# Unread matmuls in TensorE's waits, six small transfers issued by GpSimd, and a later scale exchange in a two-layer conditional FFN kernel

## The chip, the cores and the metric

The kernel runs on one core of a Trainium2 chip. The metric is device time in microseconds (us) of one execution, as a median over runs. Engines are named as the profile names them: PE (TensorE), DVE (VectorE), ACT (ScalarE), POOL (GpSimd), SP (SyncE, here only an issuer of DMAs).

## The reference

`x` is 64 batches of 64 channels by 1024 positions, in fp32. Two layers are added to it, each a small mixing followed by a matmul with a 1024x1024 weight:

```python
# layer 0: an attention over K=8 kernels makes a 64x64 matrix per batch; fp8 quantised FFN
att = softmax(gelu(gelu(cond @ W0 + b0) @ W1 + b1) @ W2 + b2)
mixed = einsum('boi,bih->boh', einsum('bk,koi->boi', att, weight), x) + (att @ bias_k)[:, :, None]
fp8_x, sx = mixed / (amax(|mixed|) / 448) in fp8;  fp8_w, sw = the same of weight.T
x = x + (fp8_x @ fp8_w) * (sx * sw) + bias
# layer 1: a grouped convolution of 9 taps plus a context column; FFN with 4-bit weights, dequantised
y = conv1d(x, weight, groups=4, padding=4) + (cond @ c_weight.T)[:, :, None] + fside[None, :, None]
x = x + y @ ((W_q - zero) * scale).T + bias
```

Both quantisations of layer 0 are over a whole tensor. Nothing can be divided by a scale before its largest absolute value is known: that of the weight (1024x1024), and that of all mixed `x`.

## The kernel before, in words

`x` is 32 tiles of 128 partitions (two batches of 64 channels) by 1024 columns, and all of them stay in the SBUF tensor `Y` (`slot(t)` is tile t). The order on each engine is the order of the code in its block, and semaphores tie the engines together. Three stages follow each other.

The opening (to about 22 us). PE computes the small MLP on `cond`; DVE makes the softmax `att` and splits it in three bf16 parts (`att_parts`). The mixing kernels `cwk` are split by DVE in three bf16 parts `wkp` (`wk_parts` counts: part 0 ready at 1, part 1 at 3, part 2 at 4), and small SBUF to SBUF transfers spread each part over 72 partitions of `wkp9`, three transfers a part. Before, SP issues six of them (parts 0 and 1, semaphore `wkp`, line L336) and GpSimd three (part 2, `wkl`, L462). 32 matmuls (L1030) make the 64x64 matrices of all batches, which ACT (three quarters) and DVE (`place_last`, L792) write into `mixw`, zeroed by DVE in four pieces. DVE also takes the largest absolute value of the eight row blocks of the first weight (`largest_w0`, L757), as `load_w0` brings them.

The scale exchange. The eight block maxima become one column (`w_part`, L827), PE turns it into a row (L1080), DVE reduces it (`w_all`, L834), a matmul with ones spreads it over the partitions (L1053), and DVE computes the scale (`scales`, L782 and L784).

The weight stage (to about 92 us) is eight cycles on DVE: quantise one block of the first weight (L729, L732, L734), take zeros off one block of the second (`less_w1`, L819), take maxima over three mixed tiles (`largest_mixed`, L804; the list `groups` says which tiles one instruction covers). Beside it GpSimd finishes the rounding (`round_w0`, L489) and the scaling (`times_w1`, L483), PE mixes tile after tile (L1047, eight passes of fp32 for two tiles) and transposes weights, and ACT evicts the mixed tiles (L581). A second exchange, over all mixed tiles, follows.

The main stage: tiles 0 to 2 by hand, then a pipelined loop. PE runs the first FFN (L1131, L1141), the convolution (L1157, 48 matmuls a tile) and the second FFN (L1167). Before the first convolution PE turns the quantised tile 2 (`turned_first_q`, L1118) and waits for the shifted copies of tile 0 (`moved_sp`, `moved_pool`, issued at L411 and L532).

## Time and profile before

| | us |
|---|---|
| median of three runs | 531.81 (529.83 to 533.81) |
| the profiled execution, its own time | 531.02 |
| its span | 528.8 |
| PE busy | 508.1 (96%) |
| DVE busy | 414.6 (78%) |
| ACT busy | 244.4 (46%) |
| GpSimd busy | 59.3 (11%) |
| mean granted TensorE clock | 0.994 |

The profile is one execution. The span runs from the first to the last instruction on the core, and the execution's own time is 2.2 us more. Busy shares are averages over all three stages: in the opening and the weight stage DVE has next to no idle time, in the main stage PE. A matmul of fp32 appears as two passes of one count each, so that one tile's mixing is four passes (x4). Durations of single matmuls contain the pipeline's latency; where many follow each other, the total divided by the count is the rate.

### The profile page before, as it was taken

How to read it: one execution, taken by the hardware profiler on the slowest of the kernel's cores; microseconds unless marked ns; L12 is line 12 of the kernel's file. 1: busy time of each engine (PE TensorE's matmuls, PEld its weight loads, DVE VectorE, ACT ScalarE, POOL GpSimd, SP SyncE). 2: the span in 40 equal slices, each digit the busy share in tenths (PEclk: the TensorE clock that was granted, in tenths of full speed). 3: DMA queues.
4: the chain of work that ended last, by engine and by line, in shares of the span. 5: the costliest groups of instructions: out<-in, count | busy, mean ns of one | idle time of the engine just before them, and what ended most of it. 6: DMA issues, size and time to landing. Idle time of an engine off the chain costs nothing.

```text
span 528.8 us, 9418 instructions
## 1 busy us (share of the span) xinstructions
PE 508.1 (96%) x3460; PEld 282.1 (53%) x3460; DVE 414.6 (78%) x524; ACT 244.4 (46%) x286; POOL 59.3 (11%) x68
## 2 busy tenths in 40 slices
PE   2999999979999999999999999999999999999997
PEld 2544454455555555555555555555555555555563
DVE  7899999966877777777777777777777777777652
ACT  3579987844444444444444444444444444442310
POOL 5276665030000000000000000000000000000000
PEclk9999999979999999999999999999999999999999
DMA  7999671244675666665556565655665666666632
GB/s 239 393 385 408 242 283 42 79 92 131 185 198 168 201 184 177 189 180 180 180 180 180 180 180 180 180 180 180 180 180 180 183 182 184 181 188 185 195 120 79
DMA packets 85650, 100.59 MB, mean 190 GB/s; under 512 B 34468, under 2 KB 67046, under 8 KB 85638
## 3 DMA queue, kind: packets, MB, share of 16 engines
q1 hardware_dynamic: 84610, 99.41, 59.6%
q0 software_dynamic: 656, 0.82, 0.9%
q10 hardware_dynamic: 372, 0.20, 0.2%
q8 instruction: 7, 0.11, 0.1%
q14 instruction: 5, 0.04, 0.0%
HBM read 58.41 MB, written 32.75 MB: 172 GB/s over the span
## 4 chain that ended last, share of the span: by engine, by line
PE 79%; DVE 11%; DMA 4%; issue 2%; SPq 1%; ACT 1%; POOL 1%; DVEq 0%; ACTq 0%; POOLq 0%
PE pair L1167 40%; PE pair L1141 19%; PE pair L1157 16%; DVE stat L804 5%; DMA work<-work 2%; DMA Y<-in_L_ffn_weight_dram 2%; PE pair L1047 1%; PE pair L1131 1%; DVE work L729 1%; DVE work L819 1%; DVE Y L819 1%; SPq L336 1%; DVE work L732 1%; POOL fixed L489 1%; DVE work L741 1%
## 5 line engine op out<-in xcount | busy, mean ns | idle before, releaser
L1167 PE MATMUL pair<-f1T,work 128*128 128x512 f16 x1024 | 231.0, 379 | 0.0
L1167 PEld LDWEIGHTS pair<-f1T,work 128*128 128x128 f16 x1024 | 98.9, 98 | 113.4
L608 ACT ACTIVATE work<-Y,consts 128x1024 bf16 (+1 forms) x29 | 33.3, 1148 | 187.0 <-DVE work L902 187.0
L921 DVE TENSOR_TENSOR work<-Y,work 128x512 f16<-128x512 f16 (+1 forms) x64 | 71.3, 1120 | 47.3 <-ACT work L641 46.2
L1141 PE MATMUL pair<-f0T,work 128*128 128x512 bf16 x464 | 104.9, 379 | 0.7 <-DMA work<-work 0.7
L1157 PEld LDWEIGHTS pair<-taps,work 128*128 128x128 f16 x1536 | 90.4, 99 | 10.0 <-issue 2.7
L1157 PE MATMUL pair<-taps,work 128*128 128x128 f16 x1536 | 93.0, 221 | 2.6 <-DMA work<-work 2.6
L934 DVE TENSOR_TENSOR Y<-pair,Y 128x512 f32 (+1 forms) x64 | 44.1, 689 | 44.9 <-PE pair L1167 44.9
L641 ACT CAST work<-Y 128x512 f16 (+1 forms) x64 | 69.7, 1138 | 18.5 <-DVE Y L911 15.6
L1141 PEld LDWEIGHTS pair<-f0T,work 128*128 128x128 bf16 x464 | 45.3, 98 | 55.7 <-DMA work<-work 1.2
L1047 PE MATMUL pair<-Y,work 128*128 128x512 f32 x128 | 62.6, 625 | 1.2 <-DVE work L792 0.8
L646 ACT CAST work<-pair 128x512 f16<-128x512 f32 x64 | 37.4, 585 | 34.9 <-PE pair L1157 33.4
L940 DVE SCALAR_TENSOR_TENSOR pair<-work,consts,fixed 128x512 f32<-128x512 f32 x64 | 48.2, 754 | 0.1
L911 DVE SCALAR_TENSOR_TENSOR Y<-pair,stat,Y 128x512 f32 (+1 forms) x64 | 45.1, 743 | 2.6 <-PE pair L1131 1.4
L928 DVE TENSOR_TENSOR work<-pair,work 128x512 f16<-128x512 f32 x64 | 41.4, 686 | 3.2 <-ACT work L646 3.1
L581 ACT ACTIVATE Y<-pair,consts 128x1024 f32<-128x1024 f32 (+1 forms) x33 | 36.0, 1093 | 13.4 <-PE pair L1047 13.4
L895 DVE SCALAR_TENSOR_TENSOR Y<-work,Y 128x1024 bf16 (+1 forms) x29 | 35.5, 1225 | 4.0
L804 DVE TENSOR_REDUCE stat<-Y 128x1 f32<-128x1024 f32 (+2 forms) x23 | 36.4, 1629 | 0.7 <-ACT Y L581 0.6
L902 DVE SCALAR_TENSOR_TENSOR work<-work,Y 128x1024 bf16<-128x1024 bf16 x29 | 35.5, 1225 | 1.2
L1047 PEld LDWEIGHTS pair<-Y,work 128*128 128x128 f32 x128 | 23.1, 196 | 23.3 <-issue 22.0
L609 ACT ACTIVATE Y<-Y,stat (+1 forms) x29 | 32.9, 1133 | 0.0
L489 POOL TENSOR_TENSOR fixed<-Y,work 128x1024 bf16<-128x1024 f32 x8 | 24.0, 3005 | 19.7 <-DVE Y L734 19.7
(153 smaller groups left out, 229.9 us busy)
## 6 DMA issues: line engine op xcount, KB each, us to landing
Y<-in_x_dram SPq DMA_DIRECT2D x64, 512.0 KB, 3.9
out_dram<-Y SPq DMA_DIRECT2D x31, 512.0 KB, 3.8
split_rows<-work SPq DMA_DIRECT2D x30, 520.0 KB, 2.6
work<-split_rows SPq DMA_DIRECT2D x30, 520.0 KB, 3.9
Y<-in_L_ffn_weight_dram SPq DMA_DIRECT2D x8, 512.0 KB, 5.7
Y<-in_L_ffn_W_q_dram SPq DMA_DIRECT2D x5, 512.0 KB, 13.2
work<-in_L_ffn_W_q_dram SPq DMA_DIRECT2D x3, 512.0 KB, 15.5
work<-work SPq DMA_DIRECT2D x8, 65.0 KB, 3.8
```

Source lines behind the costliest of these rows:

```text
L641: nc.scalar.copy(split[:, r, h:h + S, 0], v[:, r, :]).then_inc(hi_done, 1)
L646: nc.scalar.copy(y1s[n][:, 0, :, b * C:(b + 1) * C].rearrange("p r (g a) -> p g r a", g=G), ps[4 + b][:, :].rearrange("p (g r a) -> p g r ...
L804: nc.vector.tensor_reduce(stat[:, n:n + 1], part, AX.X, ALU.max, apply_absolute_value=True).then_inc(mixed_red, 1)
L911: nc.vector.scalar_tensor_tensor(out=v, in0=ps[h][:, :], scalar=acc_neg, in1=v, op0=ALU.mult, op1=ALU.add).then_inc(x1_done, 1)
L921: nc.vector.tensor_tensor(split[:, r, s, 1], v[:, r, :], split[:, r, s, 0], ALU.subtract)\
L928: nc.vector.tensor_tensor(part(1), ps[4 + b][:, :].rearrange("p (g r a) -> p g r a", g=G, r=R8), part(0), ALU.subtract).then_inc(ylo_done, 1)
L934: nc.vector.tensor_tensor(v, ps[2 + h][:, :], v, ALU.add).then_inc(res_done, 1)
L940: nc.vector.scalar_tensor_tensor(out=ps[2 + h][:, :], in0=wsum[:, c], scalar=ctxcol[:, bass.ds(t, 1)], in1=fixed[:, c], op0=ALU.mult, op1= ...
L1047: last = mm(ps[2 * (t % 2) + h][:, :], mixw[:, t, :], slot(t)[:, h * H:(h + 1) * H], start=True, stop=True)
L1141: last = mm(ps[h][:, :], qT[n][:, k, :], f0T[:, k, h * H:(h + 1) * H], start=(k == 0), stop=(k == KT - 1))
L1157: last = mm(ps[4 + b][:, g * P:(g + 1) * P], convin[:, b * G + g, h:h + S, xp], taps16[:, wp, h, g].rearrange("p r a -> p (r a)"), start=( ...
L1167: last = mm(ps[2 + h][:, :], y1s[n][:, e, k, :], f1T[:, k, h * H:(h + 1) * H], start=False, stop=(e == 1 and k == KT - 1), skip_group_chec ...
```

## The change

Seven edits. (1) Of the nine spreading transfers SP issues three (part 0) and GpSimd six (parts 1 and 2), part 1 as soon as it is ready. (2) GpSimd waits for the four attention parts before it copies the taps. (3) The load of mixed tile 1 moves ahead of the load of weight block 7. (4) `place_last` moves from behind weight block 4's maximum to behind block 1's. (5) In the exchange, PE's transpose moves from behind tile 0 to behind tile 1, its matmul with ones from the middle of tile 1 to the middle of tile 2, the transposes of zeros and scales from behind tile 1 to behind tile 2, and DVE's two sums over the taps from ahead of the row maximum to behind it. (6) In each cycle DVE takes one single tile's maximum ahead of the zeros, and a pair's behind them; before, it took the pair's and the single one's behind. PE's bias matmul goes ahead of the taps' transposes. (7) PE gets matmuls whose results nobody reads: 16, 4 and 8 of 128x128 in the opening, 4 and 10 of 128x512 before the first convolution.

```diff
-        groups = [(0, 1)] + [g for r in range(R8) for g in ((3 * r + 1, 2), (3 * r + 3, 1))]
+        groups = [(0, 1)] + [g for r in range(R8) for g in ((3 * r + 1, 1), (3 * r + 2, 2))]
@@ sync
-            for e in range(2):
-                sp.wait_ge(wk_parts, (1, 3)[e])
-                for i in range(3):
-                    sp.dma_start(wkp9[3 * i + e:KP:9, :], wkp[:, e, :]).then_inc(ld["wkp"], 16)
+            sp.wait_ge(wk_parts, 1)
+            for i in range(3):
+                sp.dma_start(wkp9[3 * i:KP:9, :], wkp[:, 0, :]).then_inc(ld["wkp"], 16)
...
             load_w0(6)
+            load_mixing(1)
             load_w0(7)
@@ gpsimd
-            pool.wait_ge(wk_parts, 4)
-            for i in range(3):
-                pool.dma_start(wkp9[3 * i + 2:KP:9, :], wkp[:, 2, :]).then_inc(ld["wkl"], 16)
+            for e in (1, 2):
+                pool.wait_ge(wk_parts, e + 2)
+                for i in range(3):
+                    pool.dma_start(wkp9[3 * i + e:KP:9, :], wkp[:, e, :]).then_inc(ld["wkl"], 16)
+            pool.wait_ge(att_parts, 4)
@@ vector
-            for r in range(1, 5):
-                largest_w0(r)
+            largest_w0(1)
             place_last()
-            for r in range(5, R8):
+            for r in range(2, R8):
                 largest_w0(r)
...
+            dve.wait_ge(w_pe, 1)
+            nc.vector.tensor_reduce(w_all, ps[7][0:1, 0:P], AX.X, ALU.max).then_inc(w_red, 1)
             dve.wait_ge(ld["convw"], 32)
...
-            dve.wait_ge(w_pe, 1)
-            nc.vector.tensor_reduce(w_all, ps[7][0:1, 0:P], AX.X, ALU.max).then_inc(w_red, 1)
...
+                if r == 0:
+                    largest_mixed(0)
+                else:
+                    largest_mixed(2 * r + 1)
                 less_w1(r)
                 if r == 0:
-                    largest_mixed(0)
-                largest_mixed(2 * r + 1)
+                    largest_mixed(1)
                 largest_mixed(2 * r + 2)
@@ tensor
+            def keep_clock(n):
+
+                for _ in range(n):
+                    mm(ps[7][:, 0:P], ident_b, ident_b, start=True, stop=True)
...
             pe.wait_ge(ident_cast, 2)
+            keep_clock(16)
             pe.wait_ge(att_parts, 4)
...
+            keep_clock(4)
+            pe.wait_ge(ld["wkp"], 48)
+            pe.wait_ge(ld["wkl"], 96)
...
-                    if t == 1 and h == 0:
+                    if t == 2 and h == 0:
                         pe.wait_ge(w_red, R8 + 2)
...
+            keep_clock(8)
             pe.wait_ge(placed_act, 3)
...
-                if t == 0:
+                if t == 1:
                     pe.wait_ge(w_red, R8 + 1)
...
+            def keep_clock_wide(n):
+
+                for _ in range(n):
+                    mm(ps[5][:, :], ident_b, f0T[:, 0, 0:H], start=True, stop=True)
...
             turned_first_q(2, 0)
+            keep_clock_wide(4)
             turned_first_q(2, 1)
+            keep_clock_wide(10)
             pe.wait_ge(taps_split, 4)
```

PE in the opening, from the transpose of the attention parts to the first transposes of zeros, before. L1030 is the mixing matrices, L1036 the taps, L1041 the bias, L1047 a half tile each, L1080 and L1053 the exchange.

```order
L1019 MATMUL pair<-small,Y 72x64
L1022 MATMUL pair<-ident,Y 8x64
L1030 MATMUL pair<-Y 128x64 x32
L1036 MATMUL pair<-ident,Y 128x128 x8
L1041 MATMUL pair<-Y,f0T 128x64
L1047 MATMUL pair<-Y,work 128x512 x2
L1080 MATMUL pair<-ident,stat 1x128
L1047 MATMUL pair<-Y,work 128x512
L1053 MATMUL pair<-stat,work 128x1
L1047 MATMUL pair<-Y,work 128x512
L1088 MATMUL pair<-small,f0T 128x8 x16
```

The same place in the changed kernel: L1010 is the unread matmul, L1043 the matrices, L1049 the bias, L1052 the taps, L1060 a half tile each, L1094 and L1066 the exchange.

```order
L1010 MATMUL pair<-small 128x128 x16
L1031 MATMUL pair<-small,Y 72x64
L1034 MATMUL pair<-ident,Y 8x64
L1010 MATMUL pair<-small 128x128 x4
L1043 MATMUL pair<-Y 128x64 x32
L1049 MATMUL pair<-Y,f0T 128x64
L1052 MATMUL pair<-ident,Y 128x128 x8
L1010 MATMUL pair<-small 128x128 x8
L1060 MATMUL pair<-Y,work 128x512 x4
L1094 MATMUL pair<-ident,stat 1x128
L1060 MATMUL pair<-Y,work 128x512
L1066 MATMUL pair<-stat,work 128x1
```

The exchange's transpose now stands behind four half tiles instead of two, its matmul with ones behind five instead of three, and three groups of unread matmuls are new.

DVE over the same time, before. L757 is a weight block's maximum, L792 the placing, L827 the column, L831 the sums over the taps, L834 the row maximum, L782 the scale.

```order
L741 MEMSET work 128x1024
L757 TENSOR_REDUCE stat<-Y 128x1 x4
L792 COPY work<-pair 64x32x16 x2
L757 TENSOR_REDUCE stat<-Y 128x1 x3
L827 TENSOR_REDUCE stat<-stat 128x1
L831 TENSOR_REDUCE consts<-work 128x9 x2
L834 TENSOR_REDUCE stat<-pair 1x1
L782 TENSOR_SCALAR stat<-pair 128x1
```

And in the changed kernel (L760 the blocks' maxima, L795 the placing, L829 the column, L831 the row maximum, L835 the taps' sums, L785 the scale).

```order
L744 MEMSET work 128x1024
L760 TENSOR_REDUCE stat<-Y 128x1
L795 COPY work<-pair 64x32x16 x2
L760 TENSOR_REDUCE stat<-Y 128x1 x6
L829 TENSOR_REDUCE stat<-stat 128x1
L831 TENSOR_REDUCE stat<-pair 1x1
L835 TENSOR_REDUCE consts<-work 128x9 x2
L785 TENSOR_SCALAR stat<-pair 128x1
```

The placing went from behind five block maxima (counting the one at row 6 of the program) to behind two, with six left behind it, and the sums over the taps changed places with the row maximum.

PE before the first convolution, before. L1131 is a tile's first FFN, L1118 the transposes of a quantised tile in halves, L1157 the convolution.

```order
L1131 MATMUL pair<-f0T,work 128x512 x16
L1188 MATMUL pair<-work 128x512
L1118 MATMUL pair<-small,work 128x128 x8
L1157 MATMUL pair<-taps,work 128x128 x48
L1131 MATMUL pair<-f0T,work 128x512 x16
```

And in the changed kernel (L1150 the FFN, L1207 the small one between, L1132 the transposes, L1138 the unread wide matmuls, L1176 the convolution).

```order
L1150 MATMUL pair<-f0T,work 128x512 x16
L1207 MATMUL pair<-work 128x512
L1132 MATMUL pair<-small,work 128x128 x4
L1138 MATMUL pair<-f0T,small 128x512 x4
L1132 MATMUL pair<-small,work 128x128 x4
L1138 MATMUL pair<-f0T,small 128x512 x10
L1176 MATMUL pair<-taps,work 128x128 x48
L1150 MATMUL pair<-f0T,work 128x512 x16
```

Between the last halves of the transposes and the convolution 4 and 10 wide matmuls are new; the rest of the order is unchanged.

## Rows read from the trace of the kernel before

**Rows 1.** The page: chain by engine, then two costly groups (busy us, mean ns, idle).

```profile
PE 79%; DVE 11%; DMA 4%; issue 2%; SPq 1%; ACT 1%; POOL 1%; DVEq 0%; ACTq 0%; POOLq 0%
...
L1167 PE MATMUL pair<-f1T,work 128*128 128x512 f16 x1024 | 231.0, 379 | 0.0
...
L489 POOL TENSOR_TENSOR fixed<-Y,work 128x1024 bf16<-128x1024 f32 x8 | 24.0, 3005 | 19.7 <-DVE Y L734 19.7
```

**Rows 2.** Chain of work in time order, 0 to 82 us: start us, us, what.

```profile
12.52 8.51 DMA Y<-in_L_ffn_weight_dram
...
21.05 1.23 DVE stat L757
...
22.89 1.66 PE pair L1047 x2
...
24.90 0.17 DVE stat L782
```

**Rows 3.** Timeline of DVE: start us, us, engine line op operands, count.

```profile
5.56 0.68 DVE L752 TENSOR_TENSOR work<-work 64x512 bf16<-64x512 f32 x1
...
12.23 4.60 DVE L757 TENSOR_REDUCE stat<-Y 128x1 f32<-128x1024 f32 x4
16.86 1.40 DVE L792 COPY work<-pair 64x512 f32<-64x512 f32 x2
18.30 2.40 DVE L757 TENSOR_REDUCE stat<-Y 128x1 f32<-128x1024 f32 x2
...
22.39 0.73 DVE L831 TENSOR_REDUCE consts<-work 128x9 f32<-128x144 f32 x2
23.15 0.28 DVE L834 TENSOR_REDUCE stat<-pair 1x1 f32<-1x128 f32 x1
...
28.21 1.22 DVE L819 TENSOR_TENSOR work<-Y,small 128x1024 f16<-128x1024 int32 x1
```

**Rows 4.** Timeline of PE, start of the program.

```profile
13.27 1.89 PE L1030 MATMUL pair<-Y 72*128 72x64 bf16 x32 [1.52 <-DMA Y<-work]
14.96 1.95 PE L1036 MATMUL pair<-ident,Y 128*128 128x128 f32 x8
...
18.37 3.75 PE L1047 MATMUL pair<-Y,work 128*128 128x512 f32 x4 [0.84 <-DVE work L792]
...
26.92 8.99 PE L1047 MATMUL pair<-Y,work 128*128 128x512 f32 x20
```

**Rows 5.** Timeline of SP: the issues of transfers.

```profile
4.39 4.44 SPq L336 DMA_DIRECT2D Y<-work  x6
...
13.80 1.00 SPq L320 DMA_DIRECT2D Y<-in_x_dram  x2
```

**Rows 6.** Line L462, GpSimd issues: ns min/median/max, starts; then us to landing.

```profile
L462 POOL DMA_DIRECT2D Y<-work x3: 565/593/632, 6.5 to 7.8; - x3
...
DMA to landing us min/median/max: 3.8/3.9/4.9
```

**Rows 7.** DMA issues at 14.4 us: operands, count, KB each, us to landing.

```profile
Y<-in_x_dram SPq DMA_DIRECT2D x1, 512.0 KB, 9.6
```

**Rows 8.** Busy time by stretch: stretch, length, busy (x), PEclk, DMA share, GB/s.

```profile
10.00:11.00 1.00, 0.00 (x0) 0.00 (x0) 0.90 (x4) 0.00 (x0) 1.00 (x4) 1.00 0.69 196
...
110.00:111.00 1.00, 0.00 (x0) 0.00 (x0) 1.00 (x2) 0.27 (x1) 0.00 (x0) 0.50 0.82 193
```

**Rows 9.** Chain of work, 117 us on: start us, us, what.

```profile
117.06 3.47 PE pair L1131 x16
...
124.68 6.09 DMA work<-work
...
137.89 2.68 PE pair L1157 x48
```

**Rows 10.** Timeline of PE ahead of the first convolution.

```profile
109.20 0.40 PE L1118 MATMUL pair<-small,work 128*128 128x128 bf16 x4 [1.00 <-DVE work L886]
112.17 4.88 PE L1157 MATMUL pair<-taps,work 128*128 128x128 f16 x48 [2.57 <-DMA work<-work]
```

More of the change, by code:

```diff
@@ L348, in _ @@
                 for t in range(2 * n + 1, 2 * n + 3):
-                    load_mixing(t)
+                    if t > 1:
+                        load_mixing(t)
                 if n == 3:
@@ L665, in _ @@
                 keep_mixed(t)
-                if t == 1:
+                if t == 2:
                     act.wait_ge(zs_mm, 1)
@@ L1022, in _ @@
             nc.tensor.transpose(ps[6][0:K, 256:320], att, ident[0:B, 0:B]).then_inc(mlp_mm, 1)
-            pe.wait_ge(ld["wkp"], 96)
-            pe.wait_ge(ld["wkl"], 48)
+            keep_clock(4)
+            pe.wait_ge(ld["wkp"], 48)
+            pe.wait_ge(ld["wkl"], 96)
             pe.wait_ge(attp_ev, 1)
@@ L1033, in _ @@
                     last.then_inc(mix_mm, 1)
+            pe.wait_ge(ld["mbk"], 32)
+            pe.wait_ge(mlp_ev, 8)
+            mm(ps[6][:, 320:384], mbk2, attT, start=True, stop=True).then_inc(mlp_mm, 1)
             pe.wait_ge(taps_made, 3)
@@ L1038, in _ @@
             last.then_inc(taps_mm, 1)
-            pe.wait_ge(ld["mbk"], 32)
-            pe.wait_ge(mlp_ev, 8)
-            mm(ps[6][:, 320:384], mbk2, attT, start=True, stop=True).then_inc(mlp_mm, 1)
             def mixed_tile(t):
@@ L1077, in _ @@
                 mixed_tile(t)
-                if t == 0:
+                if t == 1:
                     pe.wait_ge(w_red, R8 + 1)
                     nc.tensor.transpose(ps[7][0:1, 0:P], w_part, ident[:, :]).then_inc(w_pe, 1)
-                if t == 1:
+                if t == 2:
                     pe.wait_ge(ident_cast, 3)
```

## Prediction

> **What bounds the kernel now.** I read the page's chain first: PE holds 79% of it, DVE 11% and transfers 4% [rows 1]. The second FFN runs 1024 matmuls with no idle time ahead of them [rows 1], so the main loop is full and this change does not touch it. What can move is the time at which the loop starts, and two stretches decide that. The first is the opening: the chain in order of time goes through the load of the last weight block (12.52 to 21.03 us), its maximum (to 22.28), then the scale exchange through PE, and DVE has the scale at 24.90 [rows 2]. From there DVE is without a gap of note to 79 us, so each us won or lost at 24.90 arrives at the loop. The second is the first convolution, which PE starts at 112.17, released by a transfer of the shifted rows [rows 10]. All else I leave alone: the cycles in between keep their instructions.
>
> **The clock, as the rows show it.** Tile 0's four fp32 passes took 3.75 us, 0.94 each, and the two passes ahead of the matmul with ones 1.66, 0.83 each [rows 2, 4]. Two us later twenty passes took 8.99, 0.45 each [rows 4]. That is a ratio of two, the 1.2 and the 2.4 GHz level, though the granted clock reads 1.00 there. PE had gaps of 1.52 and 0.84 us earlier [rows 4]. Before the convolution the record is plain: PE idled 1.00 us, ran 0.40, idled 2.57, and the granted clock is 0.50 at 110 us [rows 8, 10]. The 48 matmuls then took 4.88 us; in the loop 48 take 2.68 [rows 9].
>
> **Part 1, the convolution.** PE's last work ahead of the wait ends at 109.20 + 0.40 = 109.6, the convolution starts at 112.17 [rows 10]. A wide matmul at full clock costs 3.47/16 = 0.217 us [rows 9]. Four take 0.87 and fit in the 1.00 us gap ahead; ten take 2.17 and end at 111.8, so they leave 0.4 us and hide in the wait for the transfer. If the clock stays up, the convolution takes 2.68 instead of 4.88: a gain of 2.20. The transfer at its head is unchanged, since GpSimd and SP issue it as before. Late next: the first FFN of tile 2 (3.47), DVE's work on its result and the 6.09 us transfer that tile 3 waits for [rows 9]. These all hang on the convolution's end and come 2.2 earlier with it, so I take the full 2.2. If the cover is gone, that is, if the clock is down when the ten start, they take twice 2.17, end at about 113.9 and cost 1.8 us.
> The Trainium skill (TensorE: Matmul & The Clock Gate, on the 56 ns that are not 53.3) gives 106.7 and 55.6 ns from start to start for 128 columns. By it the 48 would save 48 x 0.051 = 2.45 us; the rows say 2.20, and the sum goes by the rows.
>
> **Part 2, the parts' transfers.** Before, PE had everything for the matrices at 13.27 [rows 4]. GpSimd now starts on part 1 when it is ready, one DVE instruction earlier than part 2 (the 0.68 us of L752, which begins at 5.56 [rows 3]), so its first issue moves from 6.5 to about 5.9. Six issues at 0.593 put the last at 5.9 + 5 x 0.593 = 8.8. The three of before landed 3.8 to 4.9 us after issue, the last one 4.9 [rows 6]. I take 4.9, since the last was issued nearest to this one and the weight loads now follow at once on the same engines: 13.7. The bounds are 3.8 (12.6) and as much again above, 6.0 (14.8). A step of 0.4 us later than 13.27 is therefore likelier than an earlier one. The matrices take 1.89 [rows 4] and end at 15.6 (before: 15.16). The 16 and 4 unread matmuls ahead run in PE's wait and end long before.
> The Trainium skill (DMA: Bandwidth & Descriptors, "SWDGE vs HWDGE vs iDMA") says that GpSimd writes its descriptors to state from which some DVE modes lock it out, which speaks against issuing from GpSimd. The three issues' 565 to 632 ns [rows 6] show little of it; by the rule alone the landing would only be later still.
>
> **Part 3, the maxima.** DVE is now made to place behind block 1. The four maxima from 12.23 took 4.60, 1.15 each [rows 3]; with one it is done at 13.4 and waits for the matrices until 15.6, where before it had work until 16.86 and waited for nothing. Then 1.40 for the placing [rows 3] and six maxima of 1.15: 15.6 + 1.4 + 6.9 = 23.9, against 22.28. That is 1.6 later. The load could also be last: SP saves three of its six issues, 2.2 us of 4.44 [rows 5], but at 10 to 11 us the DMA engines were already 0.69 busy [rows 8], the emptiest us of that stretch, so I let the loads come only 0.5 earlier. Against that, mixed tile 1 is now ahead of block 7. Before, block 7 landed at 21.03 and tile 2, two loads behind it, at 14.4 + 9.6 = 24.0 [rows 2, 5, 7], so 1.5 a load. Block 7 lands at 21.03 - 0.5 + 1.5 = 22.0 and its maximum ends at 23.2, sooner than 23.9, so the placing decides. With all 2.2 us of earlier issue it would land at 20.3.
>
> **Part 4, the exchange.** Before it took 24.90 - 22.28 = 2.6 us, of which 1.66 was the half tile at the lower clock that PE ran between the transpose and the ones [rows 2]. Half a tile stands between them still, but of tile 2, and with PE's gaps filled I expect 0.45 a pass, 0.9: a gain of up to 0.8. DVE gives some back, since the sums over the taps (0.73) now stand behind the row maximum. Before the row maximum began 0.87 behind the column's end and took 0.28 [rows 3]; so column 24.1, row maximum 24.8 to 25.0, sums to 25.7, scale at 25.7. Against 24.90 that is +0.8. PE must have two tiles done by 24.1: matrices to 15.6, bias and taps to 18.2 (before, taps from 14.96 and bias until 0.84 ahead of 18.37, 2.6 us [rows 4]), eight unread matmuls at 4.88/48 = 0.1 each to 19.0, then eight passes. All at 0.83 they end at 25.6; if the clock rises at 22, at 24.0. Tile 2's load, 0.5 us earlier than 24.0, is in time.
>
> **Part 5, at nothing.** Taking zeros off a block 1.2 us later in a cycle is hidden by GpSimd's rounding: that takes 3.0 us [rows 1] from the same release, a single maximum and the zeros 1.15 + 1.22 = 2.4 [rows 3]. Without that cover each of eight cycles would cost up to 1.2. GpSimd's taps copies wait for the attention parts and are needed only behind the matrices and the bias, at 16.2. Without that cover they would hold tile 0, of which 23.9 hides the first us or so. Fewer small GpSimd copies beside DVE's softmax may win tenths, which DVE then only waits for longer.
>
> **The sum.** On the profiled execution's own time: 531.02 + 0.8 (opening) - 2.2 (convolution) = 529.6. The runs' median, 531.81, is 0.8 above that execution and their spread is 4 us, more than any term.
>
> **The rivals.**
> The opening costs nothing (0.28): the parts land at 12.6 and the matrices end at 14.5. Then the placing and six maxima end at 22.8, the load's own limit is 23.2, and the scale follows 1.8 behind (25.7 - 23.9), at 24.6 to 25.0: 0.3 sooner to 0.1 later, 528.5 to 528.9. For it speaks 3.8, the landing of GpSimd's first [rows 6]; against it, that the last issued landed at 4.9. The Trainium skill (DMA: Bandwidth & Descriptors, "SWDGE vs HWDGE vs iDMA") has each DMA engine take turns between its queues, so that GpSimd's transfers would not stand behind SP's weight blocks; the landings of 3.8 to 4.9 agree, in that no issue waited for whole blocks.
> The clock falls all the same (0.12), so that the change does not do what it says: the unread matmuls may not count as work, or the gap moves against them. Then 531.02 + 0.8 = 531.8, or 533.6 with 1.8 for the ten at the low level. Against it: with 4 + 10 the idle time there is 0.5 instead of 3.6 us.
> Slower (0.08), one mechanism: tile 1 ahead of the transpose while PE is at 1.2 GHz. If the parts land at 14.8 and the clock does not rise, the matrices end at 16.7, the eight unread matmuls at 20.1, tiles 0 and 1 at 20.1 + 8 x 0.83 = 26.7 and the half of tile 2 at 28.4. The ones follow, and the scale comes at 28.7, 3.8 late: 531.0 + 3.8 - 2.2 = 532.6. It decides from a scale later than 27.1, where the convolution's gain is spent. For it: before, the clock had not risen by 24 us though PE had been busy from 13.27 with one gap of 0.84 [rows 4]. Against it: that gap is now filled.
>
> **How the numbers follow.** The likeliest case, 0.52, gives 529.6 and alone reaches from 528.9 (parts at 12.8) to 530.7 (parts at 14.8, the clock risen). The first rival reaches down to 528.5. The spread of the executions before is 2 us to a side, and I add 1.3 below the lowest case. Above, 532.4 takes in the clock's fall with the ten hidden and leaves out the slower case and the ten at the low level, about 0.13 together; below it I leave 0.07. A measurement of this kernel tells about 1% (5.3 us) from no change. Faster by over 1% would need 526.5, below every case: 0.06 for an error in all of them. Slower by over 1% would need 537: 0.03. Within 1%: 0.91.
>
> **What would show it.** Right: granted clock 1.00 at 110 us and 48 matmuls in 2.7; DVE idle ahead of the placing by about 2 us; the last block's maximum ending near 23.9; the scale near 25.7. Wrong: the parts' landing before 13, passes of 0.83 us still behind 24, or a wait in the cycles where the zeros were moved, or the gain of the convolution spent in the wait for tile 3's transfer.

## Result and the profile after

The changed kernel takes 537.59 us (median of 4 runs, 536.77 to 539.59) against 532.19 for the kernel before (4 runs, 529.83 to 533.81): ratio 1.0137, 95% interval 1.0111 to 1.0164. It is slower, by 5.4 us in the medians and by 5.75 between the profiled executions (536.77 and 531.02).

Chain of work of the changed kernel, in order of time (start us, us, what). L829 is the column of block maxima, L785 the scale, L856 the column of all tiles' maxima, L621 the first work behind the second exchange, L1160 the first FFN of tile 3:

```profile
18.56 0.69 DVE work L795
...
26.88 0.17 DVE stat L829
...
28.64 0.17 DVE stat L785
...
100.33 0.19 DVE stat L856
...
102.90 0.73 ACT Y L621
...
137.16 2.97 PE pair L1160 x13
```

The chain of the kernel before at the same two places (L851 is the column of all tiles' maxima, L1141 the first FFN of tile 3):

```profile
91.59 0.19 DVE stat L851
...
130.81 3.63 PE pair L1141 x16
```

Beside these and [rows 2], three stretches account for it. The scale comes at 28.64 instead of 24.90 us: +3.74. From the scale to the column of all maxima it takes 71.69 instead of 66.69 us (24.90 to 91.59): +5.00. From there to tile 3's first FFN 36.83 instead of 39.22 (91.59 to 130.81): -2.39. The sum is +6.35. The code of the main loop behind is the same; 0.6 us of it comes back there and at the ends outside the span.

The opening on PE and DVE, and GpSimd's issues (ns min/median/max; then us to landing), against [rows 3, 4, 6]:

```profile
16.58 1.86 PE L1043 MATMUL pair<-Y 72*128 72x64 bf16 x32 [4.07 <-issue]
...
21.61 4.92 PE L1060 MATMUL pair<-Y,work 128*128 128x512 f32 x8
27.10 0.27 PE L1094 MATMUL pair<-ident,stat 128*1 128x128 f32 x1 [0.57 <-DVE stat L829]
27.20 1.09 PE L1060 MATMUL pair<-Y,work 128*128 128x512 f32 x2
```

```profile
12.52 1.15 DVE L760 TENSOR_REDUCE stat<-Y 128x1 f32<-128x1024 f32 x1
18.56 1.40 DVE L795 COPY work<-pair 64x512 f32<-64x512 f32 x2 [4.89 <-PE pair L1043]
19.99 6.85 DVE L760 TENSOR_REDUCE stat<-Y 128x1 f32<-128x1024 f32 x6
...
27.61 0.70 DVE L835 TENSOR_REDUCE consts<-work 128x9 f32<-128x144 f32 x2
```

```profile
L464 POOL DMA_DIRECT2D Y<-work x6: 562/562/630, 5.8 to 8.7; - x6
...
DMA to landing us min/median/max: 5.5/6.6/7.8
```

The six transfers landed 5.5 to 7.8 us after issue where the three of before needed 3.8 to 4.9. The matrices (L1043) start at 16.58 instead of 13.27. DVE stands idle for 4.89 us ahead of the placing (L795) and then has six maxima left.

One cycle of the weight stage, on DVE and on GpSimd. L737 is the last step of quantising, L807 a maximum, L822 the zeros, L732 the next bit mask; L492 is the rounding, L486 the scaling:

```profile
47.09 1.28 DVE L737 SCALAR_TENSOR_TENSOR Y<-Y,stat,work 128x1024 f32<-128x1024 f32 x1
48.29 1.21 DVE L807 TENSOR_REDUCE stat<-Y 128x1 f32<-128x1024 f32 x1
49.42 2.30 DVE L822 TENSOR_TENSOR Y<-Y,small 128x1024 f16<-128x1024 int32 x1
51.65 2.27 DVE L807 TENSOR_REDUCE stat<-Y 128x1 f32<-128x2048 f32 x1
53.84 0.41 DVE L732 TENSOR_SCALAR work<-work 128x1024 int16<-128x1024 int16 x1
```

```profile
48.51 2.13 POOL L492 TENSOR_TENSOR fixed<-Y,work 128x1024 bf16<-128x1024 f32 x1 [2.40 <-DVE Y L737]
51.86 1.91 POOL L486 TENSOR_TENSOR Y<-Y,small 128x1024 f16<-128x1024 f16 x1 [1.22 <-DVE Y L822]
```

The zeros take 2.30 us where they took 1.22 [rows 3], and the rounding 2.13 where its mean was 3.0 [rows 1]. The zeros end at 51.72, 1.08 behind the rounding's end at 50.64.

Before the first convolution, against [rows 8, 10]: PE's rows, and the granted clock (seventh column, PEclk) from 119 to 120 us.

```profile
118.18 2.32 PE L1138 MATMUL pair<-f0T,small 128*128 128x512 bf16 x10
120.66 3.01 PE L1176 MATMUL pair<-taps,work 128*128 128x128 f16 x48 [0.16 <-issue]
```

```profile
119.00:120.00 1.00, 1.00 (x6) 0.48 (x5) 1.00 (x3) 0.01 (x1) 0.00 (x0) 1.00 0.82 209
```

The clock holds at 1.00, and the convolution's 48 matmuls (L1176) take 3.01 instead of 4.88. The ten unread ones end at 120.50, so the convolution starts before the shifted rows have all landed (at 122.10), and the wait for them lies inside the 3.01.

### The profile page after: what moved, and what is told of

The parts are those of the page before. It is cut to its first block, busy times and chain, and to the rows that moved or that the text cites. A ratio compares the mean times of both kernels' runs of the same rounds, so it can differ in the third digit from the quotient of the medians.

```text
span 535.0 us, 9470 instructions
## 1 busy us (share of the span) xinstructions
PE 510.0 (95%) x3470; PEld 283.9 (53%) x3502; DVE 419.1 (78%) x524; ACT 244.9 (46%) x286; POOL 54.3 (10%) x71
## 4 chain that ended last, share of the span: by engine, by line
PE 76%; DVE 16%; issue 3%; DMA 2%; ACT 1%; SPq 1%; ACTq 0%; DVEq 0%
PE pair L1186 40%; PE pair L1160 18%; PE pair L1176 15%; DVE stat L807 7%; DVE work L822 2%; DMA work<-work 2%; DVE stat L760 1%; DVE Y L822 1%; DVE work L926 1%; DVE work L735 1%; PE pair L1150 1%; DMA f0T<-in_L_cond_b_dram 1%; DVE work L732 1%; SPq L412 0%; ACT work L644 0%
## 5 line engine op out<-in xcount | busy, mean ns | idle before, releaser
L1160 PE MATMUL pair<-f0T,work 128*128 128x512 bf16 x435 | 98.6, 379 | 1.8 <-DMA work<-work 0.3
L1176 PEld LDWEIGHTS pair<-taps,work 128*128 128x128 f16 x1536 | 88.3, 98 | 8.3 <-issue 0.6
L1176 PE MATMUL pair<-taps,work 128*128 128x128 f16 x1536 | 91.2, 219 | 0.2 <-issue 0.2
L1160 PEld LDWEIGHTS pair<-f0T,work 128*128 128x128 bf16 x464 | 45.3, 98 | 55.1 <-DMA work<-work 0.6
L1060 PE MATMUL pair<-Y,work 128*128 128x512 f32 x128 | 61.7, 615 | 3.5 <-DMA Y<-in_x_dram 2.8
L807 DVE TENSOR_REDUCE stat<-Y 128x1 f32<-128x1024 f32 (+2 forms) x23 | 36.8, 1625 | 0.0
L1060 PEld LDWEIGHTS pair<-Y,work 128*128 128x128 f32 x128 | 23.0, 195 | 26.0 <-issue 21.9
L492 POOL TENSOR_TENSOR fixed<-Y,work 128x1024 bf16<-128x1024 f32 x8 | 17.1, 2134 | 21.8 <-DVE Y L737 21.8
## 6 DMA issues: line engine op xcount, KB each, us to landing
Y<-in_L_ffn_W_q_dram SPq DMA_DIRECT2D x5, 512.0 KB, 14.6
```

Of the source, the lines that this page charges most:

```text
L807: nc.vector.tensor_reduce(stat[:, n:n + 1], part, AX.X, ALU.max, apply_absolute_value=True).then_inc(mixed_red, 1)
L1060: last = mm(ps[2 * (t % 2) + h][:, :], mixw[:, t, :], slot(t)[:, h * H:(h + 1) * H], start=True, stop=True)
L1160: last = mm(ps[h][:, :], qT[n][:, k, :], f0T[:, k, h * H:(h + 1) * H], start=(k == 0), stop=(k == KT - 1))
L1176: last = mm(ps[4 + b][:, g * P:(g + 1) * P], convin[:, b * G + g, h:h + S, xp], taps16[:, wp, h, g].rearrange("p r a -> p (r a)"), start=( ...
```

## Experiments

All kernels ran beside the kernel before on the same chip. Ratios are to that, with 95% intervals. "Changed" and "before" name the kernel an experiment starts from. The stations of each profiled execution, read from its timelines of PE and DVE (start in us; the last column is the difference of the two ahead of it):

| kernel | matrices | placing | column | scale | all maxima | scale to all maxima |
|---|---|---|---|---|---|---|
| before | 13.27 | 16.86 | 22.31 | 24.90 | 91.59 | 66.69 |
| changed | 16.58 | 18.56 | 26.88 | 28.64 | 100.33 | 71.69 |
| changed, old cycle | 16.99 | 18.97 | 27.29 | 29.05 | 95.76 | 66.71 |
| changed, old parts | 14.56 | 16.56 | 24.88 | 27.20 | 98.72 | 71.52 |
| before, new cycle | 14.00 | 17.53 | 22.80 | 24.50 | 96.20 | 71.70 |
| before, wide | 13.09 | 16.84 | 22.18 | 23.87 | 90.56 | 66.69 |
| before, cycle held | 14.05 | 17.63 | 23.17 | 24.86 | 101.05 | 76.19 |
| changed, loads held | 12.95 | 14.93 | 26.83 | 28.59 | 100.28 | 71.69 |
| before, new parts | 17.17 | 19.15 | 24.09 | 26.79 | 93.49 | 66.70 |
| before, unread | 13.47 | 17.00 | 22.63 | 24.32 | 90.98 | 66.66 |
| before, unread, again | 13.08 | 17.47 | 22.41 | 24.19 | 90.87 | 66.68 |
| changed, rest | 13.56 | 17.10 | 24.00 | 26.12 | 92.82 | 66.70 |
| before, early placing | 13.26 | 15.26 | 23.58 | 26.43 | 93.29 | 66.86 |
| before, early placing and unread | 14.06 | 16.06 | 24.38 | 26.07 | 92.75 | 66.68 |

The last column is 66.7 to 66.9 with the old order of a cycle and 71.5 to 71.7 with the new, whatever the opening does. The one exception is "before, cycle held", where an extra wait was put on GpSimd.

### Where the cycles' 5.0 us come from

The changed kernel with the old order in each cycle:

```diff
-        groups = [(0, 1)] + [g for r in range(R8) for g in ((3 * r + 1, 1), (3 * r + 2, 2))]
+        groups = [(0, 1)] + [g for r in range(R8) for g in ((3 * r + 1, 2), (3 * r + 3, 1))]
...
-                if r == 0:
-                    largest_mixed(0)
-                else:
-                    largest_mixed(2 * r + 1)
                 less_w1(r)
                 if r == 0:
-                    largest_mixed(1)
+                    largest_mixed(0)
+                largest_mixed(2 * r + 1)
                 largest_mixed(2 * r + 2)
```

> The changed kernel with the old order inside each cycle (zeros, pair, single) and all else changed. Theory L (port): the zeros read two SBUF tensors while GpSimd's rounding reads SBUF; whichever starts first holds the other up for its whole instruction. Zeros first: they take 1.2 us again instead of 2.2, the rounding 3.0 instead of 2.1, the next bit mask 0.9 instead of 0.4 in six cycles, a cycle 7.07 instead of 7.67, and from the scale to the end of the maxima 66.7 us instead of 71.7. Total about 5.0 below the changed kernel, near 532. Theory D (the cycles are late because mixed tiles or second-weight blocks arrive late, as a consequence of the late opening): the zeros keep 2.2 us or DVE gets idle time in their place, total near 536.5.

Measured: 532.97 us (10 runs), ratio 1.0041 (1.002 to 1.0062). A cycle of its DVE and its GpSimd (L822 zeros, L732 mask, L492 rounding, L486 scaling):

```profile
40.06 1.22 DVE L822 TENSOR_TENSOR work<-Y,small 128x1024 f16<-128x1024 int32 x1
41.19 3.40 DVE L807 TENSOR_REDUCE stat<-Y 128x1 f32<-128x2048 f32 x2
44.51 0.93 DVE L732 TENSOR_SCALAR work<-work 128x1024 int16<-128x1024 int16 x1
```

```profile
40.22 3.06 POOL L492 TENSOR_TENSOR fixed<-Y,work 128x1024 bf16<-128x1024 f32 x1 [1.11 <-DVE Y L737]
43.24 1.91 POOL L486 TENSOR_TENSOR work<-work,small 128x1024 f16<-128x1024 f16 x1
```

The zeros start first, at 40.06, and take 1.22. The rounding is recorded from 40.22 and takes 3.06, 0.93 more than the 2.13 of the changed kernel. The mask starts at 44.51 and ends at 45.44, 0.29 behind the scaling's end at 45.15. So each engine's time grows when the other was there first. Theory L holds and D falls.

The kernel before with only the new order (the same edit the other way round, its line on `groups` left out here):

```diff
...
-                less_w1(r)
                 if r == 0:
                     largest_mixed(0)
-                largest_mixed(2 * r + 1)
+                else:
+                    largest_mixed(2 * r + 1)
+                less_w1(r)
+                if r == 0:
+                    largest_mixed(1)
                 largest_mixed(2 * r + 2)
```

> The kernel before with only the new order in each cycle (single tile's maximum, zeros, pair). Theory L (port): zeros 2.2 us instead of 1.2, rounding 2.1 instead of 3.0, cycles of 7.67 instead of 7.07, total +5 us, near 536.5. Theory D (late data of the changed opening): nothing changes, as the opening is that of before; total 531 to 532.

Measured: 535.34 us (5 runs), ratio 1.0093 (1.006 to 1.0125), with the opening untouched. Zeros on DVE (L819) and the rounding on GpSimd (L489), in one cycle:

```profile
45.27 2.33 DVE L819 TENSOR_TENSOR Y<-Y,small 128x1024 f16<-128x1024 int32 x1
```

```profile
44.37 2.15 POOL L489 TENSOR_TENSOR fixed<-Y,work 128x1024 bf16<-128x1024 f32 x1 [2.40 <-DVE Y L734]
```

The rounding ends at 46.52, the zeros 1.08 later. This edit alone makes the kernel slower by 4.3 us (5 were expected), and from the scale to all maxima it takes 71.70.

Whether the two share bandwidth or shut each other out was tested by keeping them apart. The kernel before, new order, and GpSimd's rounding waits for the zeros:

```diff
                 pool.wait_ge(w_chain, 3 * r + 3)
+                pool.wait_ge(w1_less, r + 1)
                 nc.gpsimd.tensor_tensor(w0c(r), w0f[:, r, :], wz[r % 2], ALU.subtract).then_inc(w0q, 1)
```

> The kernel before with the new order in each cycle, and GpSimd's rounding made to wait until the zeros of its cycle are off. Theory L (port held for a whole instruction by whoever starts first): zeros and rounding no longer overlap, so the zeros take 1.2 us and the rounding 2.1, both at their shortest. The rounding starts 2.4 us later, GpSimd's scaling follows it, and the next cycle's bit mask on DVE now runs into the scaling: it grows from 0.4 to between 1 and 2.3 us, a cycle to between 8 and 9.1 us, from the scale to the end of the maxima 76 to 83. Rival B (the two only share bandwidth, each slowed in proportion): as the overlap is gone everything is at its shortest and a cycle is 6.6 us.

Measured: 540.96 us, one run. DVE (L730 mask, L733 the next step of the quantising, L820 zeros) and GpSimd (L490 rounding, L483 scaling):

```profile
41.14 0.46 DVE L730 TENSOR_SCALAR work<-work 128x1024 int16<-128x1024 int16 x1
41.63 2.02 DVE L733 TENSOR_SCALAR work<-work 128x1024 bf16<-128x1024 bf16 x1
...
46.02 1.22 DVE L820 TENSOR_TENSOR Y<-Y,small 128x1024 f16<-128x1024 int32 x1
```

```profile
39.18 2.14 POOL L490 TENSOR_TENSOR fixed<-Y,work 128x1024 bf16<-128x1024 f32 x1 [2.85 <-DVE work L820]
41.27 2.10 POOL L483 TENSOR_TENSOR work<-work,small 128x1024 f16<-128x1024 f16 x1
```

Zeros and rounding are both at their shortest, as expected. The stall moved, not into the mask as I had written but into the step behind it: L733 takes 2.02 instead of 0.43, starts at 41.63 while the scaling runs, and ends 0.28 behind it. A cycle is 8.2 us (41.14 to 49.34) and the stretch 76.19, both within what theory L expected; sharing would have given a cycle of 6.6. The scaling takes 2.10 here instead of 1.91; the mask was still running when it began. An instruction of 0.43 us that is slowed in proportion does not become 2.02 and end with the other engine's: B falls. The Trainium skill says just this (SBUF — State Buffer, "Who interferes with whom"): DVE instructions in a two-port mode, and those with two SBUF inputs against a GpSimd instruction that reads SBUF, contend for a port pair that GpSimd shares, and whoever starts first keeps it for the whole instruction. The traces of all three orders above agree, with 0.9 us more for the rounding, 1.1 for the zeros and 1.6 for L733.

### Where the opening's 3.7 us come from

The changed kernel with the parts' transfers of before:

```diff
-            sp.wait_ge(wk_parts, 1)
-            for i in range(3):
-                sp.dma_start(wkp9[3 * i:KP:9, :], wkp[:, 0, :]).then_inc(ld["wkp"], 16)
+            for e in range(2):
+                sp.wait_ge(wk_parts, (1, 3)[e])
+                for i in range(3):
+                    sp.dma_start(wkp9[3 * i + e:KP:9, :], wkp[:, e, :]).then_inc(ld["wkp"], 16)
@@ gpsimd
-            for e in (1, 2):
-                pool.wait_ge(wk_parts, e + 2)
-                for i in range(3):
-                    pool.dma_start(wkp9[3 * i + e:KP:9, :], wkp[:, e, :]).then_inc(ld["wkl"], 16)
+            pool.wait_ge(wk_parts, 4)
+            for i in range(3):
+                pool.dma_start(wkp9[3 * i + 2:KP:9, :], wkp[:, 2, :]).then_inc(ld["wkl"], 16)
...
```

> The changed kernel with six of the nine spreading transfers issued by SP again and three by GpSimd. Theory T (GpSimd's transfers share the DMA engines with weight blocks that SP now requests 2.2 us earlier): the transfers land near 13.3 again instead of 16.5, the matrices end near 15.2, the placing is done at 16.6, the scale is ready near 25.5 instead of 28.6, the total 3 us below the changed kernel, near 534. Rival M (the unread matmuls or the taps' wait on GpSimd delay the matrices): they still start at 16 us or later and the total stays at 536.5.

Measured: 535.68 us (5 runs), ratio 1.0086 (1.0054 to 1.0119). The matrices start at 14.56, two us earlier and not three, and the scale comes 1.4 earlier and not 3. M falls in the main: the unread matmuls and the taps' wait are still there, and the nine other kernels of the table with the old transfers, four of them with unread matmuls in the opening, start the matrices at 13.08 to 14.06. PE's rows show where the rest stayed (L1043 matrices, L1049 bias, L1060 tiles 0 and 1, L1094 the exchange's transpose):

```profile
14.56 1.89 PE L1043 MATMUL pair<-Y 72*128 72x64 bf16 x32 [2.91 <-DMA Y<-work]
17.30 0.68 PE L1049 MATMUL pair<-Y,f0T 8*128 8x64 f32 x2 [0.85 <-DMA f0T<-in_L_cond_bias_k_dram]
...
20.53 5.36 PE L1060 MATMUL pair<-Y,work 128*128 128x512 f32 x8
25.72 0.27 PE L1094 MATMUL pair<-ident,stat 128*1 128x128 f32 x1
```

The bias matmul, now ahead of the taps, waits 0.85 us for its own small load, and the two tiles ahead of the transpose take 5.36 us, so that the column, ready at 24.88 + 0.16, is transposed only at 25.72. In this kernel the later exchange costs by itself.

The changed kernel with weight blocks 3 and later requested only behind the landing of the parts:

```diff
+            sp.wait_ge(ld["wkp"], 48)
+            sp.wait_ge(ld["wkl"], 96)
             load_w0(3)
```

> The changed kernel, with SP issuing weight block 3 and all later loads only after the nine spreading transfers have landed. Theory T (weight blocks on the same DMA engines delay them): they land 3.8 to 4.9 us after issue, the matrices start at 12.6 to 13.7 instead of 16.6. Rival Q (six transfers behind each other in GpSimd's one queue are slow by themselves): the matrices start after 15.5 us as well. The total is later in both, since the last weight block comes some 5 us late.

Measured: 537.16 us, one run. GpSimd's six issues (L466):

```profile
L466 POOL DMA_DIRECT2D Y<-work x6: 565/565/632, 5.8 to 8.7; - x6
...
DMA to landing us min/median/max: 4.2/4.4/4.5
```

The same issues at the same times land after 4.2 to 4.5 us instead of 5.5 to 7.8, and the matrices start at 12.95. Only SP's later loads, the weight blocks first, were moved, so T holds and Q falls: the transfers were late because the blocks were requested early. That is one execution; the kernel below shows the reverse. The gain is spent at once, as the blocks now come late (DVE waits 1.32 and 1.95 us for the last two) and the scale is at 28.59.

The kernel before with only the new split of the transfers (the reverse of the diff above):

> The kernel before with only the shift of three transfers from SP to GpSimd (weight blocks 3 on requested 2.2 us earlier, placing behind block 4 as before). Theory T: the matrices start near 16.5 instead of 13.1 to 14.6, the placing ends near 20, the scale comes near 26.5 to 27.5, total +2 to +3 us, 533 to 534. Rival P (only the early place of the placing makes a late landing costly): DVE takes its maxima in the meantime, the scale stays within 0.5 us of 24.9, total 531.

Measured: 532.71 us (10 runs), ratio 1.0031 (1.0012 to 1.0049), +2.1 in the medians.

```profile
DMA to landing us min/median/max: 4.8/7.1/8.4
```

```profile
16.30 1.22 DVE L757 TENSOR_REDUCE stat<-Y 128x1 f32<-128x1024 f32 x1 [1.02 <-DMA Y<-in_L_ffn_weight_dram]
19.15 1.40 DVE L792 COPY work<-pair 64x512 f32<-64x512 f32 x2 [1.63 <-PE pair L1030]
20.58 3.47 DVE L757 TENSOR_REDUCE stat<-Y 128x1 f32<-128x1024 f32 x3
```

The matrices start at 17.17, and the scale comes at 26.79, 1.9 later than before. DVE fills part of the wait with maxima, but three are left behind the placing. P falls.

The kernel before with only the early placing:

```diff
-            for r in range(1, 5):
-                largest_w0(r)
+            largest_w0(1)
             place_last()
-            for r in range(5, R8):
+            for r in range(2, R8):
```

> The kernel before with only the placing moved from behind weight block 4's maximum to behind block 1's. DVE waits from 13.4 until the matrices end at 15.2 to 16, so the placing starts 1.0 to 1.3 us earlier than 16.9 but has six maxima behind it instead of three: the last ends near 23.7 and the scale is ready 1.2 to 1.7 us later than before, total +1.5, 532. If the load of the last block were the bound instead, nothing would change.

Measured: 534.27 us (10 runs), ratio 1.0072 (1.005 to 1.0094). DVE's rows:

```profile
11.89 1.15 DVE L757 TENSOR_REDUCE stat<-Y 128x1 f32<-128x1024 f32 x1
15.26 1.41 DVE L792 COPY work<-pair 64x512 f32<-64x512 f32 x2 [2.22 <-PE pair L1029]
16.70 6.85 DVE L757 TENSOR_REDUCE stat<-Y 128x1 f32<-128x1024 f32 x6
```

DVE waits 2.22 us, the column comes at 23.58 and the scale at 26.43, +1.5 as expected. The profiled execution took 532.42, also +1.4, but the median is 3.7 above that of before. Since exchange (2.85) and convolution (5.28) ran at the low clock there, I ran the same edit together with all unread matmuls:

> The kernel before with all unread matmuls and the early placing. The early placing alone cost 3.7 us in the medians, while in its profiled execution the scale came only 1.5 us late and the exchange and the convolution ran at the low clock (2.85 and 5.28 us). Theory C (the excess over 1.5 is the clock, which PE's longer idle time in the opening and before the convolution lets fall): with unread matmuls in the waits the excess goes, the exchange takes 1.7 us, the convolution 2.8, and the total is 1.2 to 1.7 us above the kernel with unread matmuls alone (528.4 to 528.6), near 530. Rival X (something else in the early placing costs): the total stays 3.5 us above it, near 532.

Measured: 531.32 us (12 runs, 529.30 to 534.37), ratio 1.0018 (0.9997 to 1.004). The exchange is 1.69 and the convolution 2.84, and the profiled execution took 529.8, but the median is 2.7 to 3.0 above the kernels with unread matmuls alone. That lies between the two theories. In both kernels the profiled execution is near the lower end of a spread of some 5 us, and over that spread the time goes with the mean granted clock of the execution. The fastest and the slowest of each:

| kernel | executions, their clock | us |
|---|---|---|
| before, early placing | 2 at 0.993 and 0.994 | 531.93 and 532.42 |
| | 3 at 0.981 | 535.79 to 536.58 |
| before, early placing and unread | 3 at 1.000 | 529.30 to 529.80 |
| | 3 at 0.987 to 0.990 | 532.63 to 534.37 |

With the unread matmuls alone no execution was below 0.994. So the clock did fall in some executions with the early placing, unread matmuls or not, which speaks for theory C's cause though not for its cure. Where it fell, and whether something else delayed PE first, no trace shows, as the traced execution is one at 1.000. A candidate is a late landing, which with the early placing has no maxima to hide behind: the matrices' start differed by 1.5 us between executions that issued the transfers alike (13.1 to 14.6). This stays open.

### What the unread matmuls and the later exchange give

The kernel before with the wide ones alone:

```diff
...
             turned_first_q(2, 0)
+            keep_clock_wide(4)
             turned_first_q(2, 1)
+            keep_clock_wide(10)
```

> The kernel before with only the 4 and 10 wide unread matmuls ahead of the first convolution. The clock holds at 1.00 where it was 0.50, the 48 matmuls take 2.7 instead of 4.9 us, and the total falls by 2.2 to 2.4 us, to about 0.996 of before. Rival: the time comes back in the wait of tile 3's first FFN, ratio 1.000.

Measured: 528.86 us (12 runs) against 531.00, ratio 0.9971 (0.9941 to 1.0000).

```profile
109.96 2.32 PE L1124 MATMUL pair<-f0T,small 128*128 128x512 bf16 x10
112.54 2.84 PE L1162 MATMUL pair<-taps,work 128*128 128x128 f16 x48 [0.26 <-issue]
```

The convolution takes 2.84 instead of 4.88 and the median is 2.1 lower. The interval just touches 1 through a single execution: one took 534.70, the other eleven 527.67 to 529.50.

One trace against one proves little for the stretch, as the landing of the shifted rows moves by 2 us from kernel to kernel. Over all fourteen it is plain: from the column of all maxima to tile 3's first FFN the five kernels without the wide matmuls take 38.9 to 40.3 us (mean 39.6), the nine with them 36.6 to 38.4 (mean 37.4). The difference of the means is 2.2.

The kernel before with all unread matmuls, on two chips (the edit above and this one):

```diff
...
             pe.wait_ge(ident_cast, 2)
+            keep_clock(16)
             pe.wait_ge(att_parts, 4)
...
+            keep_clock(4)
             pe.wait_ge(ld["wkp"], 96)
...
+            keep_clock(8)
             pe.wait_ge(placed_act, 3)
```

> The kernel before with all the unread matmuls (16, 4 and 8 in the opening, 4 and 10 ahead of the convolution) and nothing else. If those in the opening bring the clock up before 22 us, the exchange takes 1.7 us instead of 2.6 and the total is 0.9 below the kernel with the wide ones alone, near 528. If the clock in the opening comes up when it would anyway, the exchange varies between 1.7 and 2.6 as before and the total equals that of the wide ones alone, 528.9.

> The kernel before with all the unread matmuls, on the same chip as the two others: 2.0 to 2.4 us below the kernel before, and equal to the changed kernel's remainder if that remainder holds nothing else of weight.

Measured: 528.59 us (11 runs), ratio 0.9955 (0.9937 to 0.9974), and 528.36 us (12 runs), ratio 0.9962 (0.9947 to 0.9978). This is 2.0 to 2.2 us below the kernel before, and so ahead of the changed kernel too. What the small ones in the opening add to the wide ones is not resolved: 0.3 to 0.5 us between medians. From column to scale it takes 1.69 and 1.78 us. Without them the exchange took 2.59, 2.85 and 2.70 in three profiled executions and 1.70, 1.69 and 1.69 in three others, so they may make sure of something that comes by itself half of the time; three traces with them do not show it.

The changed kernel without the new transfers, the early placing and the new cycle (three of the diffs above undone in it):

> The changed kernel with the old parts' transfers, the old place of the placing and the old cycle: what is left is the later exchange, tile 1's earlier load, GpSimd's wait, the bias matmul ahead of the taps and all unread matmuls. If the port, the transfers and the early placing are all that costs, this equals the kernel before with the unread matmuls alone, 528.6. If the later exchange or tile 1's load costs on its own, it is slower: the last weight block lands 1.5 us later, its maximum ends 1 us later and the scale comes 1 us later, 529.6.

Measured: 529.47 us (12 runs), ratio 0.9983 (0.9964 to 1.0002), 1.1 above the unread matmuls alone on the same chip. DVE waits 1.79 us for the last weight block, now behind tile 1's load; PE waits for the bias's load (L1047); and the two tiles (L1058) hold the transpose:

```profile
22.74 1.22 DVE L760 TENSOR_REDUCE stat<-Y 128x1 f32<-128x1024 f32 x1 [1.79 <-DMA Y<-in_L_ffn_weight_dram]
```

```profile
16.25 0.68 PE L1047 MATMUL pair<-Y,f0T 8*128 8x64 f32 x2 [0.80 <-DMA f0T<-in_L_cond_bias_k_dram]
...
19.47 5.33 PE L1058 MATMUL pair<-Y,work 128*128 128x512 f32 x8
24.64 0.27 PE L1092 MATMUL pair<-ident,stat 128*1 128x128 f32 x1
```

The column is ready at 24.00 + 0.16, the transpose runs at 24.64, and the scale comes 1.9 us later than with the unread matmuls alone (24.19). Together the later exchange, tile 1's load and the bias's place are a loss against the unread matmuls alone, a small one; they were not taken apart.

## Why the prediction was wrong

I forecast 529.6 (527.2 to 532.4), a gain, with 0.03 for a loss of over 1%. It lost 1.4%. Of the 7.2 us between forecast and profiled execution (529.6 and 536.77) part 5 makes 5.0 and the opening 2.9 (+3.74 against +0.8); 0.2 came back in part 1 and 0.6 behind.

**Part 1, the convolution: right.** The clock held, the cover was there, and the stretch to tile 3's FFN gained 2.39 where I had 2.20; over all kernels it is 2.2, and the wide matmuls alone lower the median by 2.1. The size is closer than its working. I set 4.88, a timeline's duration, against the chain's 2.68; by timelines alone it is 4.88 against 2.84, so 2.04, and in the changed kernel 3.01, so 1.87. The rest of the 2.39 is that the convolution started 0.25 earlier behind the column and that tile 3's transfer was waited for 0.34 instead of 0.72 us.

**Part 5, the step that failed.** I priced the zeros' move at nothing because GpSimd's rounding (3.0 us) outlasts a maximum and the zeros (2.4). "Up to 1.2" a cycle stood there for the case that this cover is gone, but no rival and no chance took it up. The order of finishing was right, but I used durations as if they belonged to the instruction. 3.0 us of rounding was 2.1 of work and 0.9 of standing behind the zeros [rows 1], and with the order turned round DVE stands instead, on the chain: zeros 2.24 to 2.32 instead of 1.22, less what the bit mask gets back (0.41, once 0.60, instead of 0.9 in six cycles). The cycle measured 7.67 us against 7.07, the stretch +5.00. With the edit alone the kernel is 4.3 us slower. A hint was there to read in the trace of before: the bit mask takes 0.42 in the second cycle, where no scaling is running, and 0.92 in the third, where it starts at 40.37 and the scaling runs from 39.08 to 41.00.

**Part 2, mis-sized.** The first issue at 5.83 and the last at 8.7 are as computed. The landing was 7.8 us after the last instead of 4.9, beyond my upper bound of 6.0, and the matrices started 3.3 later than before instead of 0.4. I had noted that the weight blocks follow at once on the same engines, and made no more of it than to choose the highest landing seen, 4.9. With the blocks held back no landing is above 4.5. Those stand beside the same DVE work, so nothing there shows DVE holding up GpSimd's issues.

**Part 3, right in kind.** Placing and six maxima took 1.40 + 6.85 as computed (1.4 + 6.9), so the error of part 2 went through in full: the last maximum ends at 26.84 against my 23.9. DVE's wait was 4.89 us, not 2. The early placing costs 1.5 us in the scale even with the old landing, 0.3 of it in an exchange that was slower by itself (2.85 against 2.59).

**Part 4, right in number, partly by luck.** From the last maximum's end to the scale it took 1.8 us (26.84 to 28.64), as forecast; the passes ran at the full level by then (1.09 for two). The path was another. I read the 0.87 us ahead of the row maximum of before as PE's, and most of it was DVE's own sums over the taps (22.39 + 0.73, row maximum at 23.15 [rows 3]). With the sums moved behind, the row maximum began 0.36 behind the column and not 0.7 to 0.9, and DVE did not end the exchange with its sums but waited 0.32 for PE's ones (L1066). In two kernels the two tiles ahead of the transpose did hold it, by 0.5 and 0.7 us, which is the slower rival in small.

**The rivals.** The first, with 0.28, leaned in part on GpSimd's transfers not standing behind SP's weight blocks. They landed after 5.5 to 7.8 us with blocks 3 and later requested beside them and after 4.2 to 4.5 with those held back, so they were held up by them. The slower one gave the scale at 28.7, and it came at 28.64, but that is coincidence: its mechanism (tile 1 at the low clock) did not come, as the transpose waited for the column (26.88) and not for the tiles. The loss was a later landing and the order of a cycle, and the second had no rival at all. The chances of 0.91 for within 1% rested on cases that all kept part 5 at nothing.

## What to carry to other kernels

Where DVE and GpSimd both work on SBUF, read the duration of an instruction together with what the other engine ran at its start: if it grows by what was left of the other's, the time is a wait, and a new order moves it to whoever comes second. Put the wait on the engine that is off the chain. A small transfer that an engine waits for should be weighed against the large loads whose requests the same edit moves forward. Unread matmuls pay where PE waits with a long run of matmuls behind the wait. In the traces with the wide ones the convolution ran at the full level whether the wait left behind them was 0.16 us (the changed kernel) or 1.59 us (unread, again); that the clock holds in every execution does not follow.

## What the runs showed of the hardware that I had not expected

The wait between DVE and GpSimd is exclusive: 0.43 us of work was recorded as 2.02, ending 0.28 behind GpSimd's instruction. It shows as a longer instruction and not as idle time. GpSimd's six small transfers needed 4.2 to 4.5 us to land when SP requested weight blocks 3 and later only afterwards, and 5.5 to 7.8 (in another kernel 4.8 to 8.4) with weight blocks in SP's queue, although their issues took the same 562 to 637 ns. Being in another queue did not shield them.
